# Two key tiles of half 8 go to the softmax denominators one by one on TensorE, without a sum on GpSimd

## The chip, the cores and the metric

The kernel runs on one core of a Trainium2 chip. The metric is the device time of one execution in microseconds (us), the median of several runs. The core has a matrix engine (TensorE, PE in the rows; its weight loads are PEld), a vector engine (VectorE, DVE), an activation engine (ScalarE, ACT), GpSimd (POOL) and a queue of transfers on SyncE (SP). Each runs its own instructions in program order and waits for the others by semaphores.

## What is computed

A gated cross-attention block and a gated feed-forward block over x (4 batches of 1024 rows, 512 columns), with 16 heads of 32 columns:

```
q = rope(layernorm(x));  k = rope(ctx);  v = ctx
scores = q . k / sqrt(32) + alibi bias
attn   = softmax(scores);  out = attn . v
x = x + tanh(g_xattn) * out
x = x + tanh(g_ffn) * ffn(layernorm(x))      # quantized gate, up and down projections
```

The softmax is computed as exponentials P, a numerator (P times v) and a denominator (the sum of P over the 1024 keys), which divides at the end. The change is in how the denominator is summed.

## The kernel before

The attention part works on 16 units of one batch and four heads, each cut in two **halves** of 512 queries: 32 halves, number 0 to 31. The 1024 keys of a half are 8 **tiles** of 128 keys, number 0 to 7, and each tile has a **step**: s = 0 to 7 in half hf, global number g = 8*hf + s. The order of the work is written out by hand: a class Step says for every g which jobs of which half each engine does, and every engine's program walks over the same list.

In a step TensorE computes the scores of this tile for four heads (L1066, f16, four column blocks of 32), the scores of an earlier-to-be-used tile for the row maxima (L1053, ten steps ahead, in two units of 1024 columns), and the numerator of the tile before (L1128, fp32). In the trace a step starts with the row `L1066 ... x8`. ScalarE turns scores into P (L1308, one instruction a head, into a ring of six P buffers). VectorE reduces the two units of scores to maxima (L1533); a bank of PSUM that it has not yet read holds back TensorE's next L1053 into that bank.

The denominator of a half is a product of summed P with a small matrix of zeros and ones, `pick`, which sums over the 128 keys of a tile (`denominators`, L1099, 16 fp32 matmuls, each two instructions in the trace, so x32). What is summed first:

- Sum 0: GpSimd adds tiles 0 and 1 at step 1 (L2186), then a transfer with addition from GpSimd's queue adds tile 2 (L2162, issued at step 3). TensorE takes it at step 6.
- Sum 2: GpSimd adds tiles 3 and 4 at step 4, a transfer adds tile 5 (step 6). TensorE takes it at step 10, that is step 2 of the next half.
- Sum 1: GpSimd adds tiles 6 and 7 at step 7. TensorE takes it at step 9, step 1 of the next half, ahead of that step's numerator.

In a half for which `direct(hf)` is true, sum 1 doesn't exist: TensorE takes tile 6 out of its P buffer at step 7 (behind the numerator) and tile 7 at step 9 (ahead of the numerator). Before the change these are the even halves from 18 to 28.

Beside the sums GpSimd does the rotary embedding (`rope`: L2010, L2017, L2018, L2028) for the unit after next, adds x to the output (L2172, step 5), works out deviations (L2055) and, in later halves, parts of the weight quantization. ScalarE copies the denominator out at step 3 of the next half (L1345); that row marks each half once. TensorE transposes the half's results at step 4 of the next half (L1135, L1139).

In the names, Ps are the buffers of the sums, P those of the exponentials, and g_sum, a_exp, pe_den count GpSimd's sums, ScalarE's exponentials and TensorE's denominators. ScalarE may write a P buffer again when what read its tile is done: for tiles 6 and 7 that is g_sum, and pe_den in a direct half.

Of the kernel before, what the change touches and what calls it, by code (L numbers as in the profile page):

```python
# [113 lines left out]

def direct(hf):

    return hf % 2 == 0 and 18 <= hf < 30


def sums(hf):  # L120

    return 2 if direct(hf) else 3


def den_steps(hf):

    return {0: 6, 6: 7, 7: 9, 2: 10} if direct(hf) else {0: 6, 1: 9, 2: 10}
# [1112 lines left out]
def scalar_program(e, K):  # L1240
# [51 lines left out]
    def exponent(hf, kt, h):  # L1292
        pb = (8 * hf + kt) % NP
        n = 8 * hf + kt
        e.wait_ge(K.pe_score, score_no(hf, kt, h))
        if h == 0 and n >= NP:
            m = n - NP
            e.wait_ge(K.pe_pv, m + 1)
            hm, km = m // 8, m % 8
            if hm < NHALF - 1 and km > 5 and direct(hm):  # L1300
                e.wait_ge(K.pe_den, den_no(hm, km))
            elif hm < NHALF - 1 and km % 3 < 2:
                e.wait_ge(K.g_sum, sum_no(hm, (0, 2, 1)[km // 3]))
            elif hm < NHALF - 1:
                e.wait_ge(K.d_acc[km // 3], 16 * hm + 16)
            else:
                e.wait_ge(K.v_sum, m // 2 - 4 * (NHALF - 1) + 1)
        e.activation(K.Pb[pb][:, h, :], K.score[h % 2], ACT.Exp, scale=SCALE / (QPOW * KPOW)).then_inc(K.a_exp, 1)  # L1308
# [951 lines left out]
```

## Time and profile before

| | |
|---|---|
| median of 3 runs | 1728.41 us (1728.23 to 1728.67) |
| the profiled execution, its own time | 1728.73 us |
| its span, first to last instruction | 1726.9 us |
| mean granted TensorE clock | 0.979 |
| attention part, by the denominators' copies (L1345) | 89.72 us (half 0) to 894.43 us (half 31) |
| step 1 of half 8 to step 1 of half 10 | 266 to 320 us |

The page of the profile gives busy shares over the whole span, of which the attention part is the first half; what binds in the attention part must be read from its own stretch. TensorE's busy time hides how matmuls overlap, so the distance between the starts of its rows says more than their durations.

### The profile page before, as it was taken

The page shows a single profiled execution, that of the slowest core. Times are in us where ns is not written, and L with a number is a line of the kernel's source. Part 1 is how long each engine was busy: PE and PEld are TensorE (multiplying, and loading weights), DVE is VectorE, ACT ScalarE, POOL GpSimd, SP SyncE. Part 2 cuts the span into 40 slices and gives each one's busy share as a digit, 9 for nine tenths or more (in the row PEclk, how much of TensorE's full clock was granted, in tenths as well). Part 3 has the DMA queues.
Part 4 walks back from the last instruction along what each step waited for, and adds up shares of the span by engine and source line. Part 5 has one row for each costly group of instructions (what it writes and reads, how often), then busy time and mean ns, then how long its engine had stood idle before and what let it go on. Part 6 is the DMA issues. An engine that isn't in the chain of part 4 may idle for free. (4 is left out here: it accounts for less than half of the span.)

```text
span 1726.9 us, 42023 instructions
## 1 busy us (share of the span) xinstructions
PE 1593.0 (92%) x17245; PEld 692.4 (40%) x17245; DVE 1443.0 (84%) x2039; ACT 1206.7 (70%) x1938; POOL 810.1 (47%) x493
## 2 busy tenths in 40 slices
PE   3999999999999999999969999999999950999999
PEld 0244444344334444444435444444444420444444
DVE  7899999999999989889857999868899989755541
ACT  3788888888889889998753332329996988754450
POOL 4799999999999999997830110200000000000000
PEclk9999999999999999999999999999999985999999
DMA  6678888888789797878478898649998999976661
GB/s 157 161 155 181 166 174 179 174 170 173 157 177 181 156 177 168 171 152 161 99 173 226 255 270 262 213 161 326 343 350 266 323 356 385 287 256 226 216 214 61
DMA packets 376337, 365.11 MB, mean 211 GB/s; under 512 B 217776, under 2 KB 288816, under 8 KB 368208
## 3 DMA queue, kind: packets, MB, share of 16 engines
q1 hardware_dynamic: 367216, 297.41, 61.7%
q0 software_dynamic: 8928, 65.02, 18.7%
q8 instruction: 135, 2.21, 0.5%
q14 instruction: 58, 0.48, 0.1%
HBM read 150.93 MB, written 95.42 MB: 143 GB/s over the span
## 5 line engine op out<-in xcount | busy, mean ns | idle before, releaser
L1533 DVE TENSOR_REDUCE cm<-quad 128x1 f16<-128x1024 f32 x512 | 600.3, 1214 | 52.6 <-PE quad L1053 52.1
L1308 ACT ACTIVATE P<-quad 128x512 f32<-128x512 f32 x1024 | 556.8, 598 | 119.6 <-PE quad L1066 108.7
L2186 POOL TENSOR_TENSOR Ps<-P,P 128x2048 f32<-128x2048 f32 x87 | 405.9, 4666 | 60.5 <-ACT P L1308 60.5
L1066 PE MATMUL quad<-QA,KA 101*32 101x512 f16 x4096 | 360.1, 384 | 8.1 <-ACT P L1308 6.1
L1053 PE MATMUL quad<-KA,QA 100*32 100x512 f16 x4096 | 334.5, 390 | 32.9 <-DMA QA<-S 16.9
L1128 PE MATMUL quad<-P,cg 128*32 128x512 f32 x2048 | 264.7, 592 | 0.0
L1158 PE MATMUL quad<-x_hl,Wg 128*128 128x512 f16 (+1 forms) x1200 | 248.9, 371 | 0.6 <-DVE x_hl L1852 0.6
L1158 PE MATMUL quad<-x_hl,Wu 128*128 128x512 f16 x1152 | 248.8, 380 | 0.0
L1219 PE MATMUL quad<-Wd,oh 128*128 128x512 f16 x768 | 228.8, 380 | 0.9 <-ACT oh L1502 0.9
L1066 PEld LDWEIGHTS quad<-QA,KA 101*32 101x32 f16 x4096 | 104.9, 95 | 247.0 <-ACT P L1308 218.8
L1053 PEld LDWEIGHTS quad<-KA,QA 100*32 100x32 f16 x4096 | 104.3, 96 | 181.3 <-DVE cm L1533 88.8
L1158 PEld LDWEIGHTS quad<-x_hl,Wg 128*128 128x128 f16 x1200 | 117.3, 98 | 132.7 <-issue 1.5
L1158 PEld LDWEIGHTS quad<-x_hl,Wu 128*128 128x128 f16 x1152 | 112.6, 98 | 136.0
L1392 ACT ACTIVATE ev<-quad 128x1024 f32<-128x1024 f32 x89 | 90.1, 1013 | 106.7 <-PE quad L1158 100.6
L1219 PE MATMUL quad<-Wd,ol 128*128 128x512 f16 x384 | 145.8, 380 | 0.2 <-DVE ol L1967 0.2
L2129 POOL TENSOR_TENSOR wq<-wl,wsc 128x512 f32<-128x512 f32 x36 | 43.1, 1197 | 211.9 <-DVE wl L1688 211.9
L1837 DVE TENSOR_REDUCE mxt<-ev 128x1 f32<-128x1024 f32 x89 | 108.1, 1215 | 35.9 <-ACT ev L1392 35.5
L1988 DVE SCALAR_TENSOR_TENSOR xr<-quad,qs,xr 128x512 f32<-128x512 f32 x32 | 23.9, 750 | 110.3 <-PE quad L1219 105.3
L1219 PEld LDWEIGHTS quad<-Wd,oh 128*128 128x128 f16 x768 | 75.1, 98 | 91.9 <-ACT oh L1502 1.4
L1502 ACT ACTIVATE oh<-oq 128x512 f16<-128x512 int16 x96 | 60.0, 625 | 67.3 <-DVE oq L1962 47.0
L1099 PE MATMUL quad<-Ps,pick 128*32 128x128 f32 x2912 | 96.4, 273 | 7.6 <-POOL Ps L2186 4.3
L1099 PEld LDWEIGHTS quad<-Ps,pick 128*32 128x32 f32 x2912 | 80.3, 110 | 56.5 <-issue 45.1
(181 smaller groups left out, 1964.7 us busy)
## 6 DMA issues: line engine op xcount, KB each, us to landing
Ps<-P POOLq DMA_DIRECT2D x62, 1024.0 KB, 8.0
gate_scratch<-ev SPq DMA_DIRECT2D x48, 512.0 KB, 3.9
gt<-gate_scratch SPq DMA_DIRECT2D x48, 512.0 KB, 5.3
ud<-up_scratch SPq DMA_DIRECT2D x96, 256.0 KB, 3.6
up_scratch<-ev SPq DMA_DIRECT2D x42, 512.0 KB, 4.4
x_words<-up_scratch SPq DMA_DIRECT2D x39, 512.0 KB, 7.8
gated_scratch<-gq SPq DMA_DIRECT2D x48, 256.0 KB, 4.1
gd<-gated_scratch SPq DMA_DIRECT2D x96, 128.0 KB, 4.2
```

Of the source, the lines that this page charges most:

```text
L1053: mm = e.matmul(K.bank(use, c)[j:j + 32, :], K.QA[p % 2][0:100, 4 * qc + qt, h, j:j + 32], K.KA[p % 2][0:100, 4 * c:4 * c + 4, h, :], star ...
L1066: mm = e.matmul(K.score[h % 2][j:j + 32, :], K.KA[p % 2][0:101, kt, h, j:j + 32], K.QA[p % 2][0:101, 4 * qc:4 * qc + 4, h, :], start=True, ...
L1099: mm = e.matmul(K.den[32 * h:32 * h + 32, :], K.pick[:, qt, :], src[:, h, 128 * qt:128 * qt + 128], start=n == order[0] and qt == 0, stop= ...
L1128: mm = e.matmul(K.num[32 * h:32 * h + 32, :], K.cg[(p + 1) % 4][:, kt, 32 * h:32 * h + 32], K.Pb[before.g % NP][:, h, :], start=kt == 0, s ...
L1158: mm = e.matmul(K.quad[z][:, o:o + w], W(part, c), K.x_hl[:, x, c0:c0 + w], start=n == 0, stop=n == 11)
L1219: mm = e.matmul(ps, o[k][:, ot, sl], K.Wd[r][:, ot, :], start=ot == m == 0, stop=ot == OT - 1 and m == 2)
L1308: e.activation(K.Pb[pb][:, h, :], K.score[h % 2], ACT.Exp, scale=SCALE / (QPOW * KPOW)).then_inc(K.a_exp, 1)
L1392: e.activation(dst, src, ACT.Copy).then_inc(K.a_ev, 1)
L1502: e.activation(K.oh[ch % 2][:, ot, :], K.oq[n % 2][:, :], ACT.Copy).then_inc(K.a_oh, 1)
L1533: e.tensor_reduce(cm[:, col:col + 1], K.quad[UNIT["max", hm, u] % 2][:, :], AX.X, ALU.max).then_inc(K.v_max, 1)
L1837: e.tensor_reduce(K.mxt[:, col:col + 1], src, over, ALU.max, apply_absolute_value=True).then_inc(K.v_mx, 1)
L2186: e.tensor_tensor(K.Ps[n][:, :, :], K.Pb[(st.g - 1) % NP][:, :, :], K.Pb[st.g % NP][:, :, :], ALU.add).then_inc(K.g_sum, 1)
```

## The change

Half 8 becomes a direct half too.

```diff
 def direct(hf):
 
-    return hf % 2 == 0 and 18 <= hf < 30
+    return hf == 8 or hf % 2 == 0 and 18 <= hf < 30
 
 
 def sums(hf):
 
     return 2 if direct(hf) else 3
 
 
 def den_steps(hf):
 
     return {0: 6, 6: 7, 7: 9, 2: 10} if direct(hf) else {0: 6, 1: 9, 2: 10}
```

On TensorE, at step 7 of half 8, the difference is one group of 16 matmuls more (P_94 holds tile 6, cg is v; the rows count a matmul once):

```order
 L1066 MATMUL quad<-QA_86,KA_88 32x512 x4
 L1128 MATMUL quad<-P_94,cg_84 32x512 x4
+L1099 MATMUL quad<-P_94,pick 32x128 x16
 L1066 MATMUL quad<-QA_86,KA_88 32x512 x8
 L1053 MATMUL quad<-KA_89,QA_87 32x512 x12
```

The group stands behind the numerator of tile 6 and ahead of the scores of half 9's first tile.

On TensorE two steps later, at step 1 of half 9, a group reads another buffer (Ps_98 is sum 1, P_141 holds tile 7, P_90 is tile 0 of half 9):

```order
 L1053 MATMUL quad<-KA_89,QA_87 32x512 x4
 L1066 MATMUL quad<-QA_86,KA_88 32x512 x4
-L1099 MATMUL quad<-Ps_98,pick 32x128 x16
+L1099 MATMUL quad<-P_141,pick 32x128 x16
 L1128 MATMUL quad<-P_90,cg_84 32x512 x4
 L1066 MATMUL quad<-QA_86,KA_88 32x512 x8
```

Its place and its size stay; what it waits for is no longer GpSimd's sum.

On GpSimd, at step 7 of half 8, the sum goes (Ps_99 is sum 2, t is the rotary embedding, Ps_97 is sum 0 of half 9):

```order
 L2162 DMA Ps_99<-P_93 128x2048
 L2028 TENSOR_TENSOR t_136<-t_136,t_137 128x1024
-L2186 TENSOR_TENSOR Ps_98<-P_94,P_141 128x2048
 L2010 TENSOR_TENSOR t_135<-xn,cos 128x1024
 L2186 TENSOR_TENSOR Ps_97<-P_90,P_91 128x2048
```

All behind it on GpSimd moves up by one place. VectorE, ScalarE and SyncE have the same instructions in the same order.

## Rows read from the trace of the kernel before

**Rows 1.** The page, part 1: busy us, share of the span, instructions
```profile
PE 1593.0 (92%) x17245; PEld 692.4 (40%) x17245; DVE 1443.0 (84%) x2039; ACT 1206.7 (70%) x1938; POOL 810.1 (47%) x493
```

**Rows 2.** Windows of 26 and 27 us over half 8 and half 9
```profile
core 0: us, PE busy (x) PEld busy (x) DVE busy (x) ACT busy (x) POOL busy (x), PEclk, DMA share, GB/s
261.00:287.00 26.00, 24.90 (x421) 10.37 (x417) 24.08 (x34) 22.58 (x44) 25.20 (x11) 1.00 0.96 187
287.00:313.00 26.00, 24.64 (x417) 10.51 (x413) 25.17 (x43) 21.05 (x40) 24.49 (x19) 1.00 0.71 156
```

**Rows 3.** Timeline of TensorE, end of half 8: start us, us, instruction, [idle before]
```profile
283.90 1.04 PE L1099 MATMUL quad<-Ps,pick 128*32 128x128 f32 x32
284.77 0.61 PE L1066 MATMUL quad<-QA,KA 101*32 101x512 f16 x8
...
287.79 0.60 PE L1066 MATMUL quad<-QA,KA 101*32 101x512 f16 x8
...
289.08 0.40 PE L1053 MATMUL quad<-KA,QA 100*32 100x512 f16 x4 [0.25 <-DVE cm L1533]
...
290.82 0.61 PE L1066 MATMUL quad<-QA,KA 101*32 101x512 f16 x8
...
294.55 0.61 PE L1066 MATMUL quad<-QA,KA 101*32 101x512 f16 x8
```

**Rows 4.** Timeline of TensorE in direct half 20, steps 7 to 1
```profile
601.69 0.61 PE L1066 MATMUL quad<-QA,KA 101*32 101x512 f16 x8
...
604.62 1.04 PE L1099 MATMUL quad<-P,pick 128*32 128x128 f32 x32
605.50 0.61 PE L1066 MATMUL quad<-QA,KA 101*32 101x512 f16 x8
...
608.16 0.61 PE L1066 MATMUL quad<-QA,KA 101*32 101x512 f16 x8
```

**Rows 5.** Timeline of GpSimd, half 8's last sum and half 9
```profile
287.88 4.62 POOL L2186 TENSOR_TENSOR Ps<-P,P 128x2048 f32<-128x2048 f32 x1 [1.09 <-ACT P L1308]
292.46 2.39 POOL L2010 TENSOR_TENSOR t<-xn,cos 128x1024 f32<-128x1024 f32 x1
294.81 4.56 POOL L2186 TENSOR_TENSOR Ps<-P,P 128x2048 f32<-128x2048 f32 x1
...
301.81 0.79 POOL L2162 DMA_DIRECT2D Ps<-P  x1
...
315.21 4.82 POOL L2186 TENSOR_TENSOR Ps<-P,P 128x2048 f32<-128x2048 f32 x1
```

**Rows 6.** Timeline of TensorE in half 9: its two waits
```profile
310.88 1.08 PE L1099 MATMUL quad<-Ps,pick 128*32 128x128 f32 x32 [1.04 <-DMA Ps<-P]
...
320.08 1.08 PE L1099 MATMUL quad<-Ps,pick 128*32 128x128 f32 x32 [0.47 <-POOL Ps L2186]
```

**Rows 7.** Timeline of ScalarE, exponentials of half 9's tile 1
```profile
292.80 1.10 ACT L1308 ACTIVATE P<-quad 128x512 f32<-128x512 f32 x2
```

**Rows 8.** Timeline of GpSimd in direct half 20
```profile
611.32 4.59 POOL L2186 TENSOR_TENSOR Ps<-P,P 128x2048 f32<-128x2048 f32 x1 [2.62 <-ACT P L1308]
```

**Rows 9.** The sums' buffers, 299.5 to 313 us: transfer to landing
```profile
DMA to landing us min/median/max: 8.9/8.9/8.9
```

**Rows 10.** Timeline of VectorE in the same stretch
```profile
289.53 2.35 DVE L1533 TENSOR_REDUCE cm<-quad 128x1 f16<-128x1024 f32 x2
...
312.31 0.87 DVE L1766 BATCH_NORM_STATS2 st<-x2s 128x6 f32<-128x128 f32 x4 [0.55 <-POOL x2s L2172]
```

**Rows 11.** ScalarE's copies of the denominators, halves 7, 8, 23 and 24
```profile
273.78 0.28 ACT L1345 ACTIVATE denT<-quad 128x128 f32<-128x128 f32 x1
299.50 0.28 ACT L1345 ACTIVATE denT<-quad 128x128 f32<-128x128 f32 x1
...
695.61 0.28 ACT L1345 ACTIVATE denT<-quad 128x128 f32<-128x128 f32 x1
721.82 0.28 ACT L1345 ACTIVATE denT<-quad 128x128 f32<-128x128 f32 x1
```

## The prediction

> **What bounds the kernel now.** I began with the busy shares of the page [rows 1]. They put TensorE first (92%) and GpSimd at 47%, and say nothing useful here: GpSimd has work only in the attention part. So I went to windows of the stretch around the change [rows 2]. There GpSimd is busy for 25.20 of 26.00 us over half 8 and 24.49 over half 9, VectorE for 24.08 and 25.17, TensorE for 24.90 and 24.64. The reader should see three engines that are nearly full, each of which can be late only a few tenths of a microsecond before it holds up another. Sizes of instructions alone then decide nothing. What counts is how the few gaps between them open and close, and the timelines give those.
>
> TensorE at the end of half 8 [rows 3]: step 7 runs from 284.77 to 287.79 (3.02 us), step 0 of half 9 from there to 290.82 (3.03 us), step 1 to 294.55 (3.73 us). A group of denominators takes 284.77 - 283.90 = 0.87 us between starts (not the 1.04 us of the row, which is the overlapped duration), so step 1 without its group is 2.86 us. What is a step with no wait at all? Step 0 of direct half 20 has no group in it and takes 608.16 - 605.50 = 2.66 us [rows 4]. TensorE thus loses 0.36 us in step 7, 0.37 in step 0 and 0.20 in step 1, and the row at 289.08 says to whom: to VectorE, which has not yet read a bank of maxima [rows 3].
>
> GpSimd [rows 5]: it waits 1.09 us for tile 7 before the sum at 287.88, which takes 4.62 us. From then on there is no gap: the rotary embedding at 292.46, sum 0 of half 9 at 294.81, the transfer with addition at 301.81, sum 1 of half 9 from 315.21 to 320.03. Two of these are waited for in half 9 by TensorE [rows 6]: it stands 1.04 us for the transfer (at 310.88) and 0.47 us for sum 1 (at 320.08). So through half 9 it is GpSimd that sets the end, which is what makes a sum taken off it interesting.
>
> **The change, part by part.**
>
> *Removed: sum 1 of half 8 on GpSimd, 4.62 us [rows 5].* Little of that can be passed on. The rotary embedding behind it can move up by nearly all of it, but sum 0 of half 9, the next but one, needs the exponentials of half 9's tile 1. Before, ScalarE ended them at 292.80 + 1.10 = 293.90 [rows 7], so GpSimd, which began at 294.81, was 0.91 us late and no more. In direct half 20, where the sum is already gone, the same instruction at 611.32 indeed waits, 2.62 us, for ScalarE [rows 8], and begins 611.32 - 608.16 = 3.16 us after TensorE's step 1 [rows 4, 8]. I use this 3.16. With TensorE's step 1 where it was (290.82) sum 0 would start at 293.98, 0.83 us earlier. This is the ceiling of the gain.
>
> *Added: one group of denominators on TensorE at the end of step 7.* The same group out of a P buffer takes 605.50 - 604.62 = 0.88 us in half 20 [rows 4]. It waits for nothing: the numerator just ahead of it reads the same tile. Step 0 then starts at 288.67 rather than 287.79. A TensorE that is later no longer waits for VectorE: 0.37 us of the delay is absorbed in step 0 and 0.20 in step 1. The 0.36 lost in step 7 lies ahead of the group and stays. So step 1 starts at 290.82 + 0.88 - 0.37 = 291.33, and step 2 at 294.55 + 0.88 - 0.57 = 294.86: 0.31 us late. If none of it were absorbed it would be 0.88, if all were, 0.
>
> *Changed source at step 1:* the group there reads tile 7 and not the sum. Same size, same place, and no row shows TensorE standing for the sum there; nothing.
>
> *The release of P buffers for ScalarE* now comes from TensorE (at about 288.7 and in step 1) and not from GpSimd at 292.50. These buffers are written again at steps 4 and 5 of half 9, later than either. Nothing, and if that cover were gone it would cost only what TensorE's groups are late.
>
> *Sum.* Sum 0 of half 9 starts at 291.33 + 3.16 = 294.49, against 294.81: 0.32 us earlier. What follows it on GpSimd has no gap, so the transfer goes out at 301.49. It landed 8.9 us after issue [rows 9]; the wait at 310.88 ends at 310.56. TensorE, which was there at 310.88 - 1.04 = 309.84, is there at 310.15 and still waits 0.41. The delay of TensorE has thus vanished in a wait that was there anyway, and that is why it costs nothing in the end. VectorE is pushed in step 0 by less than TensorE (it started on that step's maxima at 289.53, 1.74 us behind TensorE's start), and waits 0.55 us for GpSimd's L2172 at 312.31 [rows 10], which takes up the push. At 320.08 TensorE waits for sum 1, now 0.32 earlier; even with no gain at the transfer TensorE could be there at 320.08 - 0.47 = 319.61, ahead of 319.76 [rows 6]. From there all engines stand 0.32 us earlier and do the same work as before, to the end. The profiled execution would take 1728.73 - 0.32 = 1728.41 us; the median of the runs shown, 1728.41, is 0.32 below that execution, so the prediction is 1728.41 - 0.32 = **1728.09 us**, rounded 1728.1. Measurement tells 0.2% (3.5 us) from no change, so this is no change.
>
> *A rule weighed.* The row: between the groups of denominators TensorE's steps follow each other at 2.66 us, one after another, in which nothing waits [rows 4], so 0.88 us more of matmuls that find no gap are 0.88 us later. The Trainium skill, page "Perfetto Trace Analysis", section "Identifying the Most-Contended Engine", says that a matmul share is no measure of TensorE's headroom, and that the share of weight loads is one. Here that is 40%. Read so, TensorE would have room and the added group would cost nothing; the sum by the page would be the ceiling, -0.83 us, and 1727.58. I weigh this against the row as the third rival below.
>
> **The rivals.**
>
> *Whole sum passed on (3%).* If GpSimd alone set the pace, 4.62 us would go: 1723.8 us. For it: GpSimd is the fullest engine over half 8 [rows 2] and has no gap for 32 us behind the sum [rows 5]. Against it: the 293.90 of the exponentials [rows 7] and the 2.62 us that half 20 waits [rows 8].
>
> *The exponentials come later than I reckon (12%), the slower side.* The removal gains only while TensorE's step 1 starts before 294.81 - 3.16 = 291.65. If the delay is not absorbed (VectorE falls late with TensorE, and releases its banks later) step 1 starts at 291.70 and the gain is -0.05. More than that: direct half 24 lasts 721.82 - 695.61 = 26.21 us, and half 8 lasts 299.50 - 273.78 = 25.72 [rows 11]. If being direct is what costs these 0.49 us, GpSimd's sum 0 is as late and the result is 1728.41 + 0.49 = 1728.90. Against it: halves around 24 have more work of weights on GpSimd and VectorE, so the comparison is loose.
>
> *TensorE's added group is hidden in whole (17%).* Its step 1 starts where it did, and GpSimd gains the ceiling: 1728.41 - 0.83 = 1727.58. This needs VectorE to be the one that paces steps 7 to 1 with more to spare than the 0.57 us that I count.
>
> *Nothing (20%).* GpSimd's own instructions differ by more than the gain: the same L2186 takes 4.56 and 4.82 us within half 9 [rows 5], as it meets other work or not. A shift of its neighbours can eat 0.3 us: 1728.4.
>
> **How the numbers follow.** My forecast has 46%; with the four rivals that is 98%. The last 2% are for a shift that I can't place in the long transfer-heavy part behind the attention. Cases from 1727.58 to 1728.90 hold 95%; the medians' own scatter (0.44 us between runs) and the rounding of the cases add some tenths on each side: 1726.9 to 1729.2. The faster side by over 0.2% (below 1724.95) needs the whole sum passed on, 3%; slower by over 0.2% (above 1731.9) has only the unplaced remainder, 2%; no change 95%.
>
> **What the profile of the changed kernel would show.** A group `P,pick` at about 287.8 and the next step at 288.67; no wait for VectorE at 289; step 2 of half 9 at 294.86. GpSimd idle for about 3 us around 291, for ScalarE, and sum 0 of half 9 at 294.49. The transfer's wait in TensorE about 0.4 us, ending near 310.56; the wait for sum 1 near 319.76, and the copy of half 9's denominators 0.3 us earlier than before. The prediction is wrong if sum 0 starts after 294.81, if the shift at 320 us is not the shift at the end, or if GpSimd doesn't wait at all in the gap.

## The result, and the profile after

| | before | changed |
|---|---|---|
| median of the timed runs | 1728.81 us (1727.58 to 1731.75, 15 runs) | 1732.53 us (1729.64 to 1735.82, 15 runs) |
| ratio, 95% interval | | 1.0019 [1.0013, 1.0026] |
| profiled execution, own time and span | 1728.73 and 1726.9 us | 1731.29 and 1729.5 us |

The changed kernel is 3.7 us slower by the medians, and the interval of the ratio does not reach 1. The forecast was 1728.1 us, no change, range 1726.9 to 1729.2. The three runs shown ahead of the prediction were close to each other (0.44 us); over 15 runs the same kernel spreads by 4.2 us, so the measured effect is clear and not large.

Half 8 itself did what was predicted. The two traces stand 0.43 us apart when half 8 begins (copy of half 7's denominators at 274.21, before 273.78 [rows 11]), so all positions below are to be read against that. Timeline of TensorE in the changed kernel, steps 7 to 1, the answer to [rows 3]:

```profile
285.20 0.61 PE L1066 MATMUL quad<-QA,KA 101*32 101x512 f16 x8
...
288.22 1.04 PE L1099 MATMUL quad<-P,pick 128*32 128x128 f32 x32
289.09 0.60 PE L1066 MATMUL quad<-QA,KA 101*32 101x512 f16 x8
...
291.76 0.61 PE L1066 MATMUL quad<-QA,KA 101*32 101x512 f16 x8
...
295.29 0.61 PE L1066 MATMUL quad<-QA,KA 101*32 101x512 f16 x8
```

The new group takes 289.09 - 288.22 = 0.87 us, and step 2 starts at 295.29, which is 294.55 + 0.43 + 0.31: TensorE is 0.31 us late, as worked out. GpSimd, the answer to [rows 5]:

```profile
294.91 4.59 POOL L2186 TENSOR_TENSOR Ps<-P,P 128x2048 f32<-128x2048 f32 x1 [3.86 <-ACT P L1308]
```

It waits for ScalarE and starts 3.15 us after step 1 (3.16 predicted), 0.33 us earlier than before once the 0.43 are taken off. TensorE's two waits in half 9, the answer to [rows 6]:

```profile
310.78 1.08 PE L1099 MATMUL quad<-Ps,pick 128*32 128x128 f32 x32 [0.26 <-DMA Ps<-P]
...
320.28 1.08 PE L1099 MATMUL quad<-Ps,pick 128*32 128x128 f32 x32 [0.49 <-POOL Ps L2186]
```

The second is at 320.08 + 0.43 - 0.23: the place where the gain was to arrive shows 0.23 us of the 0.32. Up to here there is no loss at all.

The loss is in halves that the change doesn't touch. The copies of the denominators give the length of each half. ScalarE in the changed kernel, halves 11, 12, 17, 18, 19 and 20:

```profile
379.75 0.28 ACT L1345 ACTIVATE denT<-quad 128x128 f32<-128x128 f32 x1
406.19 0.28 ACT L1345 ACTIVATE denT<-quad 128x128 f32<-128x128 f32 x1
...
538.78 0.30 ACT L1345 ACTIVATE denT<-quad 128x128 f32<-128x128 f32 x1
565.59 0.28 ACT L1345 ACTIVATE denT<-quad 128x128 f32<-128x128 f32 x1
592.34 0.28 ACT L1345 ACTIVATE denT<-quad 128x128 f32<-128x128 f32 x1
619.94 0.28 ACT L1345 ACTIVATE denT<-quad 128x128 f32<-128x128 f32 x1
```

The same rows of the kernel before:

```profile
379.42 0.28 ACT L1345 ACTIVATE denT<-quad 128x128 f32<-128x128 f32 x1
405.14 0.28 ACT L1345 ACTIVATE denT<-quad 128x128 f32<-128x128 f32 x1
...
537.77 0.29 ACT L1345 ACTIVATE denT<-quad 128x128 f32<-128x128 f32 x1
563.99 0.28 ACT L1345 ACTIVATE denT<-quad 128x128 f32<-128x128 f32 x1
590.75 0.28 ACT L1345 ACTIVATE denT<-quad 128x128 f32<-128x128 f32 x1
616.66 0.28 ACT L1345 ACTIVATE denT<-quad 128x128 f32<-128x128 f32 x1
```

Half 12 lasts 26.44 us against 25.72, half 18 26.81 against 26.22, half 20 27.60 against 25.91: together 3.0 us. TensorE stands in these halves for the transfer with addition that completes sum 0. Its timeline in the changed kernel, halves 12 and 20:

```profile
391.23 1.08 PE L1099 MATMUL quad<-Ps,pick 128*32 128x128 f32 x32 [1.19 <-DMA Ps<-P]
...
604.15 1.08 PE L1099 MATMUL quad<-Ps,pick 128*32 128x128 f32 x32 [1.57 <-DMA Ps<-P]
```

Neither wait is in the trace of before. Halves 18 and 20 last as long as in before, within 0.04 us, in copy_before and in few (few is described below and loses no time); half 18 is 0.37 us longer in pool_only. Half 12 is no sign of the change: few, which has the time of before, has the wait too, and its half 12 lasts 26.75 us (pool_only: 26.84). TensorE in few:

```profile
390.80 1.08 PE L1099 MATMUL quad<-Ps,pick 128*32 128x128 f32 x32 [1.51 <-DMA Ps<-P]
```

So single halves of single traces have to be read with care. Still, why do transfers far behind the edit land later? Nothing in their data flow has changed. What has changed for everything behind half 8 is its place in the instruction stream, and the page says how that stream reaches the core: by transfers of its own. The row of queue 8 of the page, part 3, of the kernel before:

```profile
q8 instruction: 135, 2.21, 0.5%
```

and of the changed kernel:

```profile
q8 instruction: 136, 2.23, 0.5%
```

2.21 MB in 135 packets is 16 KB a packet. TensorE has 2 x 17245 rows, matmuls and weight loads [rows 1], which makes 64 bytes for each and 256 instructions for a packet, if the packets are TensorE's. They are by their rhythm: from 89.72 to 894.43 us the trace has 102 packets of this queue beside 25958 matmuls and weight loads, from 894.43 to 1400 us 19 beside 4701, so 254 and 247 instructions a packet, while the time between packets goes from 7.9 to 26.6 us. (Another instruction queue, q14, has 58 packets before and after.) TensorE passes 421 + 417 matmuls and loads in 26 us [rows 2], so 256 instructions are some 7.9 us, and 64 more instructions bring every later fetch some 2.0 us forward against the work around it. Both times are estimates from those rows. The idea can be tested: by 64 instructions that do nothing, anywhere ahead.

A simpler way from instructions to time can be ruled out at once: TensorE does not stand for its own instructions. Of its waits over 0.15 us between 85 and 900 us, each one in the traces of before and of the changed kernel ends with a semaphore of another engine or of a transfer.

### The profile page after: what moved, and what is told of

The parts are those of the page before. It is cut to its first block and busy times, and to the rows that moved or that the text cites. A ratio compares the mean times of both kernels' runs of the same rounds, so it can differ in the third digit from the quotient of the medians.

```text
span 1729.5 us, 42085 instructions
## 1 busy us (share of the span) xinstructions
PE 1596.5 (92%) x17277; PEld 694.6 (40%) x17277; DVE 1443.5 (83%) x2039; ACT 1207.3 (70%) x1938; POOL 806.0 (47%) x492
## 5 line engine op out<-in xcount | busy, mean ns | idle before, releaser
L1533 DVE TENSOR_REDUCE cm<-quad 128x1 f16<-128x1024 f32 x512 | 600.3, 1214 | 56.6 <-PE quad L1053 55.9
L2186 POOL TENSOR_TENSOR Ps<-P,P 128x2048 f32<-128x2048 f32 x86 | 401.4, 4667 | 67.5 <-ACT P L1308 67.5
```

Source lines behind the costliest of these rows:

```text
L1533: e.tensor_reduce(cm[:, col:col + 1], K.quad[UNIT["max", hm, u] % 2][:, :], AX.X, ALU.max).then_inc(K.v_max, 1)
L2186: e.tensor_tensor(K.Ps[n][:, :, :], K.Pb[(st.g - 1) % NP][:, :, :], K.Pb[st.g % NP][:, :, :], ALU.add).then_inc(K.g_sum, 1)
```

## The experiments

Kernels of one group ran on one chip, beside the kernel before; the groups ran on different chips. The theories by their letters: A, scatter of the landings between executions alone; B, a cause in the change, B1 the missing sum, B2 the added group or its place in the stream; F, the phase of TensorE's instruction fetches, which the added 64 instructions shift; T, the 0.88 us of TensorE's time in half 8.

### One half of the change at a time

**copy_before**: no edit. **after_again**: the changed kernel, no edit.

> The kernel before, unchanged, timed against itself. It tells how far a ratio of two identical kernels can stand from 1, and gives a second trace, in which the waits of TensorE for the transfers with addition can be set against those of the first. Theory A (the change costs nothing at its own place, and the 3.7 us between the medians come from transfers that land at different times in different executions): ratio within 0.9985 to 1.0015, and the waits of TensorE for the transfers sum to 2 to 6 us, in other halves than in the first trace. Theory B (the change itself makes it slower): ratio within 0.9995 to 1.0005, waits as in the first trace, 3.1 us.

> The changed kernel again, unchanged. Theory A (scatter of the landings): ratio between 0.999 and 1.002, and the halves that are longer than before in its trace are not 12, 18 and 20 again. Theory B (a cause in the change): ratio 1.0013 to 1.0026 as measured, and the same halves 12, 18 and 20 are longer by 0.6 to 1.7 us.

**pool_only** (the changed kernel; the denominators of half 8 leave out tile 6, and ScalarE does not wait for its buffer; an excerpt):

```diff
 def den_steps(hf):
+    if hf == 8:
+        return {0: 6, 7: 9, 2: 10}
```

> Half 8 without the sum of tiles 6 and 7 on GpSimd, and without the added group on TensorE (tile 6 is left out of the denominators of half 8). Account of the prediction: sum 0 of half 9 starts 0.83 us earlier than before, median 0.8 us below before. Theory A: ratio 0.998 to 1.001. Theory B1 (what costs is the sum that is missing on GpSimd, by shifting its transfers against those of SyncE's queue): 1.0013 to 1.0026. Theory B2 (what costs is the added group on TensorE or its place in the instruction stream): 0.9995.

**pe_only** (the changed kernel; GpSimd still makes the sum, which only ScalarE waits for, before it writes the buffers again; an excerpt):

```diff
 def sums(hf):
-    return 2 if direct(hf) else 3
+    return 2 if direct(hf) and hf != 8 else 3
```

> Half 8 with both groups on TensorE as after the change, but GpSimd still makes the sum, which nothing reads. Account of the prediction: TensorE 0.31 us late at step 2 of half 9, taken up by its wait of 1.04 us for the transfer unless GpSimd is late too: 0 to +0.3 us. Theory B1 (missing sum on GpSimd costs): ratio 1.000 to 1.0002. Theory B2 (added group on TensorE or its place in the instruction stream): 1.0013 to 1.0026.

| kernel | TensorE instructions added | median, us | ratio [95%] |
|---|---|---|---|
| before, beside them | 0 | 1729.52 | |
| copy_before | 0 | 1728.94 | 0.9996 [0.9988, 1.0005] |
| pool_only | 0 | 1729.20 | 0.9996 [0.9987, 1.0005] |
| after_again | 64 | 1731.66 | 1.0012 [1.0003, 1.0021] |
| pe_only | 64 | 1732.25 | 1.0020 [1.0009, 1.0031] |

The copy bears out that the comparison finds no difference where there is none. Its trace was expected to repeat the waits of before if theory B holds, and did not: TensorE waits 4.1 us in all for the transfers between 85 and 900 us and not 3.1, and its halves 10, 11 and 22 are 0.35 to 0.49 us longer. So the landings do scatter between executions of one kernel. As the whole cause theory A falls: the intervals of after_again and pe_only do not reach 1. The sum on GpSimd is not the cause (B1 falls): with it gone and TensorE's count unchanged, nothing is lost. With it kept and the group added, the loss is there. (In pe_only's trace one wait for a transfer, 2.73 us in half 12, is followed by a granted clock of 0.57 from 393 to 397 us, and that half lasts 29.62 us.) pool_only also confirms the ceiling of the gain at its place. GpSimd in pool_only:

```profile
294.32 4.57 POOL L2190 TENSOR_TENSOR Ps<-P,P 128x2048 f32<-128x2048 f32 x1 [3.35 <-ACT P L1312]
```

Its half 8 begins at 274.12, so the sum starts 20.20 us behind that, before 294.81 - 273.78 = 21.03: 0.83 us earlier, exactly the 0.83 of the prediction. In the medians this gain can't be told from nothing (1729.20 beside 1729.52). Of after_again's trace the expectation was too strict: half 18 is longer again (26.80), half 12 and half 20 only by 0.28 and 0.30 us. What returned more closely was not the halves but some of the landings, below.

### Is it the time of the added group, or its 64 places in the stream?

**pad64**: the kernel before, with 16 small fp32 matmuls in the idle time at the start, 64 instructions.

```diff
     mm.then_inc(K.pe_bias, 1)
+    for i in range(16):
+        e.matmul(K.quad[3][0:32, 512:544], ident[:, 0:32], ident[:, 0:32], start=True, stop=True)
```

> The kernel before, with 64 more TensorE instructions (16 small fp32 matmuls, 32 weight loads and 32 matmuls) in the idle time at the very start, where TensorE waits for its first operands; half 8 as before. Theory F (the added group moves all later TensorE instructions by 64 places in their stream, so that the fetches of 16 KB, 256 instructions each, meet other transfers with addition): from half 13 on the landings are those of the changed kernel (sum 0 of half 18 in 9.0 us and not 7.0, sum 2 of half 15 in 7.6 and not 9.7, sum 2 of half 29 in 9.0 and not 7.3), and the ratio is 1.000 to 1.002. Theory T (the 0.88 us of TensorE in half 8 do the harm): landings as before, ratio 0.9995 to 1.0005.

**few**: the kernel before, with as much TensorE time in half 8's place, in 8 instructions.

```diff
     for st in STEPS:
+        if st.g == 72:
+            e.wait_ge(K.a_exp, score_no(9, 0, 0) - 2)
+            for i in range(4):
+                e.matmul(K.score[0][0:32, :], K.KA[0][0:100, 0, 0, 0:32], K.QA[0][0:100, 0:4, 0, :], start=True, stop=True)
```

> The kernel before, with TensorE kept busy for about 0.85 us ahead of the scores of half 9's first tile by 4 f16 matmuls of 512 columns (8 instructions in place of 64), whose result is overwritten. Theory F: landings as in the kernel before, ratio 0.9995 to 1.0005, at most +0.3 us locally. Theory T: as the changed kernel, 1.001 to 1.0025.

**after_pad192** and **after_pad256**: the changed kernel with the loop of pad64, 48 and 64 matmuls.

> The changed kernel with 192 more TensorE instructions in the idle time at the start, so that behind half 8 the stream is 256 places later than in the kernel before: one fetch more, and the same phase. Theory F: from half 9 on the landings are those of the kernel before (sum 0 of half 18 in 7.0 us), and the ratio 0.998 to 1.001, unless the halves 1 to 8, whose phase is now 192 places off, lose something of their own. Theory T: 1.001 to 1.0025, as the changed kernel.

> The changed kernel with 256 more TensorE instructions at the start: the phase of the fetches is everywhere as in the changed kernel. It is the control for what the padding itself costs. Theories F and T both: 1.001 to 1.0025, landings as in the changed kernel. If the padding costs by itself, more than that.

| kernel | added ahead of half 9 | median, us | ratio [95%] |
|---|---|---|---|
| before, beside them | 0 | 1729.26 | |
| few | 8 | 1729.11 | 0.9999 [0.9990, 1.0008] |
| pad64 | 64 | 1733.61 | 1.0018 [1.0009, 1.0026] |
| after_pad256 | 256 + 64 | 1732.67 | 1.0014 [1.0005, 1.0022] |
| after_pad192 | 192 + 64 = 256 | 1731.88 | 1.0011 [1.0002, 1.0019] |

The pair pad64 and few is the core of the study. pad64 leaves half 8 alone, adds 64 idle instructions at the very start, and has the whole loss. few puts about the same time of work in the very place (its half 8 lasts 26.03 us, the changed kernel's 26.04) and has none. Theory T falls. What pad64's trace, one execution of 1730.40 us, does not show is the loss in the same halves. Its halves 18 and 20 last as long as in before, within 0.04 us, and the first transfer of half 18 landed in 7.5 us where 9.0 was expected; the longer ones are half 2 (by 1.12 us) and half 5 (by 0.51). The expected landings of half 15 (7.6) and half 29 (9.1) came.

The traces show what the count does to a landing. The second transfer of half 29 (sum 2) is far from any edit and from the halves that wait. For it, the traffic in the 7 us from its issue, of the kernel before (packets, MB, share of 16 engines; KB, us to landing):

```profile
q0 software_dynamic: 144, 1.05, 73.3%
q1 hardware_dynamic: 298, 0.26, 10.9%
...
Ps<-P POOLq DMA_DIRECT2D x1, 1024.0 KB, 7.3
```

and of the changed kernel:

```profile
q0 software_dynamic: 143, 1.05, 73.2%
q1 hardware_dynamic: 292, 0.26, 10.8%
q8 instruction: 1, 0.02, 0.8%
...
Ps<-P POOLq DMA_DIRECT2D x1, 1024.0 KB, 9.0
```

The data traffic is the same; there is one packet of instructions more, and the landing is 1.7 us later. The packet is not new: in before it starts 7.3 us after the issue, when the transfer has landed, and in the changed kernel 7.0 us after it. pad64, the same window:

```profile
q8 instruction: 1, 0.02, 0.8%
Ps<-P POOLq DMA_DIRECT2D x1, 1024.0 KB, 9.1
```

Over all of the first 14 traces (all but those of the last section of experiments) this one transfer takes, by what is added ahead of it: 0 or 8 instructions (before, copy_before, pool_only, few) 7.2 to 7.4 us; 256 (after_pad192, direct_2_8, direct_10_16) 7.3; 64 (after, after_again, pe_only, pad64, direct_10) 8.7 to 9.1; 320, that is 64 and one whole fetch (after_pad256), 9.1; 128 (pad128) 7.0. Others follow the same classes, in either direction: the first transfer of half 30 takes 7.5 to 7.7 and 8.5 us, the second of half 15 8.4 to 9.7 and 7.6 to 7.7. The landing repeats every 256 instructions. How can a packet of 16 KB among 1 MB cost up to 2 us? The Trainium skill, page "DMA: Bandwidth & Descriptors", section "Why a DMA increments its semaphore by 16 and not by 1", says that for a transfer from GpSimd's queue all 16 engines count the semaphore up, each behind its own data, and that only the full 16 means that all has landed. The traces agree: the 15th of the 16 increments of this transfer comes 7.0 us after the issue in before and in the changed kernel alike, the 16th at 7.3 and at 9.0. One part in 16 is late. That it is late because the packet stands ahead of it on the same engine is argued from this, not shown: the traces don't say which engine an increment or a packet belongs to.

A packet in the window is no rule by itself. The first transfer of half 18 in before has one too, 6.75 us after its issue, and lands in 7.0 us; in the changed kernel the packet starts at 6.98 and the landing is 9.0:

```profile
q8 instruction: 1, 0.02, 1.0%
Ps<-P POOLq DMA_DIRECT2D x1, 1024.0 KB, 7.0
```

What seems to count is when it comes. Of the 868 transfers in the 14 traces, which took 6.7 to 11.6 us (median 8.1), the 62 in which a packet of queue 8 starts 3 to 6 us after the issue all took 8.4 us or more (median 9.3).

Do later landings make the time? The attention part, from the copy of half 0's denominators to that of half 31's, follows TensorE's waits for the transfers (between 85 and 900 us): from 806.2 us with 2.0 us of waits (direct_2_8) and 804.7 with 3.1 (before) to 810.4 with 8.5 (pad128), correlation 0.89 over the 14 traces. But the traces do not separate the kernels as the medians do. With 0 or 8 instructions added the waits are 3.1, 4.1, 4.2 and 5.0 us, with 64 added 3.6, 3.7, 6.0, 6.0 and 6.3.

after_pad192 gave the landings of before from half 9 on, as theory F says, but not the time. Two things blur it: halves 4 and 8, now in another phase, are 1.24 and 0.67 us longer than in before beyond what the change adds, and in its trace TensorE's clock rises late, so that half 0 ends at 91.81 us and not at 89.72. Windows of after_pad192 (busy us and count of TensorE, its weight loads, VectorE, ScalarE and GpSimd, then the granted clock, the DMA share and GB/s):

```profile
40.00:50.00 10.00, 8.35 (x64) 1.12 (x64) 9.81 (x13) 2.00 (x2) 9.75 (x7) 0.50 0.63 159
50.00:60.00 10.00, 9.28 (x84) 2.85 (x88) 8.02 (x8) 4.87 (x9) 3.13 (x2) 0.50 0.87 200
```

and of the kernel before:

```profile
40.00:50.00 10.00, 8.34 (x64) 1.12 (x64) 9.81 (x13) 2.00 (x2) 9.84 (x6) 1.00 0.63 157
50.00:60.00 10.00, 8.30 (x92) 2.54 (x96) 8.98 (x8) 5.39 (x10) 3.65 (x3) 1.00 0.83 201
```

and of after_again, without any padding, and after_pad256, with the longest:

```profile
50.00:60.00 10.00, 9.66 (x84) 2.89 (x88) 8.02 (x7) 5.26 (x9) 2.72 (x2) 1.00 0.97 207
50.00:60.00 10.00, 9.00 (x104) 2.56 (x96) 8.64 (x8) 6.49 (x13) 3.73 (x3) 0.77 0.91 212
```

From 50 to 60 us TensorE gets through 84 matmuls in after_pad192 where it got through 92 in before. The padding is not the reason: after_again without padding gets through 84 too, after_pad256 through 104. The traces record the rise to the full level at 54.0 to 61.0 us, early or late with padding and without it, so it belongs to the single execution. (The 1.00 of before in the first of these windows is no record: the trace of before has none ahead of 55.5 us. 64 matmuls take 8.34 us there and 8.35 beside a 0.50, so TensorE was at its lower level in both.) Whether the halves in another phase explain the ratio of after_pad192 stayed open, and it was replaced by kernels without padding.

### The phase restored without padding, and moved

```diff
 def direct(hf):
-    return hf % 2 == 0 and 18 <= hf < 30
+    return hf in (2, 4, 6, 8) or hf % 2 == 0 and 18 <= hf < 30     # direct_2_8
+    return hf in (10, 12, 14, 16) or ...                           # direct_10_16
+    return hf == 10 or ...                                         # direct_10
```

pad128 is pad64 with 32 matmuls.

> Halves 2, 4, 6 and 8 direct: four groups of 64 TensorE instructions more, so that from half 9 on the stream is 256 places later, one whole fetch, and the fetches have the phase of the kernel before. Theory F: landings from half 13 on as in the kernel before (sum 2 of half 29 in 7.3 us, sum 0 of half 30 in 7.6); ratio 0.998 to 1.0010, below the 1.0012 to 1.0019 of the changed kernel. Theory T (each group on TensorE costs by itself, what half 8 alone cost): four times 0.0012 to 0.0019, ratio 1.005 to 1.008.

> Halves 10, 12, 14 and 16 direct in place of 8: the phase of the fetches is that of the kernel before up to half 9 and from half 17 on. Theory F: landings from half 17 on as in the kernel before, ratio 0.998 to 1.001. Theory T: 1.005 to 1.008.

> Half 10 direct in place of half 8: the same 64 instructions, 16 steps later. Theory F: landings as in the changed kernel from half 13 on, ratio 1.0005 to 1.002. A theory by which half 8 is special (its deviations on GpSimd and aggregates on VectorE in half 9): ratio 0.9995 to 1.0005.

> The kernel before with 128 more TensorE instructions in the idle time at the start, half a fetch. Theory F says that the time depends on the phase and not which way: between 0.998 and 1.003, with landings that are neither those of before nor those of the changed kernel. If padding at the start costs by itself in proportion to its length, it is above the 1.0018 of 64 instructions.

| kernel | added, from where | median, us | ratio [95%] |
|---|---|---|---|
| before, beside them | 0 | 1729.45 | |
| direct_2_8 | 64, 128, 192, from half 9 on 256 | 1729.74 | 1.0004 [0.9994, 1.0013] |
| direct_10 | 64 from half 11 on | 1732.42 | 1.0016 [1.0008, 1.0025] |
| direct_10_16 | 64 to 192 in halves 11 to 16, then 256 | 1733.47 | 1.0030 [1.0007, 1.0052] |
| pad128 | 128 everywhere | 1734.37 | 1.0032 [1.0021, 1.0043] |

Four groups like the one of the change, in direct_2_8, cost less than one alone in direct_10, 1729.74 against 1732.42 us on the same chip, and no difference to before is measured. Under theory T the ratio would be 1.005 to 1.008. Half 8 is not special either, half 10 does the same. direct_10_16 missed its expectation. Its landings are those of before from half 17 on and its halves 17 to 30 last as long, but its halves 12 and 14, in the phases between, last 27.23 and 26.87 us against 25.72, where their own added groups account for 0.32 each. So a phase is not good or bad by itself; what counts is which transfers the fetches meet while it lasts. (One of its twelve executions took 2433.69 us and one 1755.30, for which there is no trace; the median does not feel them, but the second is in the ratio and widens its interval.) pad128 costs more than pad64, as theory F allows; a cost of the padding by its length would do that too, but then after_pad256, with 256 idle instructions, should cost more than the changed kernel, and it does not (1.0014).

### By which wait it reaches the time

Three phases again, with TensorE taking sum 0 at step 7 and not at 6 in every half but the last, so that a late landing is covered:

```diff
-    return {0: 6, 6: 7, 7: 9, 2: 10} if direct(hf) else {0: 6, 1: 9, 2: 10}
+    return {0: 7, 6: 7, 7: 9, 2: 10} if direct(hf) else {0: 7, 1: 9, 2: 10}
```

> The kernel before, with TensorE taking sum 0 of every half at step 7 and not at step 6 (the last half aside), 2.7 us later, so that a transfer that lands in 9.0 us and not in 7.0 is still there in time. Theory F (late landings reach the time through TensorE's wait for sum 0 at step 6): the waits for transfers, 3 to 4.5 us in sum before, fall below 1 us, the time falls by 1 to 3 us: ratio 0.998 to 0.9995. If landings cost in another way, 0.9995 to 1.001.

> The changed kernel with sum 0 taken at step 7 in every half. Theory F: it loses nothing to the other phase of the fetches, and is within 1 us of late_before, ratio 0.998 to 0.9998. If the loss of the changed kernel comes by another way than TensorE's wait for sum 0, it stays 2 to 3 us above late_before.

> The kernel with 128 more TensorE instructions at the start, the slowest phase seen (1.0032), with sum 0 taken at step 7. Theory F: within 2 us of late_before, ratio 0.998 to 1.0005 (the throttled clock of the start may cost up to 1 us). By another way: 1.002 to 1.003.

| phase | sum 0 at step 6, us | at step 7, us | ratio [95%] at 7 | TensorE's waits in the trace, 85 to 900 us, for transfers, at 6 and at 7 | for VectorE's L1533 |
|---|---|---|---|---|---|
| before | 1729.45 | 1736.89 | 1.0039 [1.0026, 1.0051] | 3.1 and 0 us | 7.4 and 21.9 us |
| changed | 1732.53 | 1737.38 | 1.0052 [1.0039, 1.0065] | 6.0 and 0 | 7.4 and 21.9 |
| 128 added | 1734.37 | 1735.52 | 1.0038 [1.0026, 1.0050] | 8.5 and 0 | 7.8 and 21.9 |

The kernel before took 1729.92 us beside the three at step 7. Those at step 6 are from other groups. late_before ran five times, of which one took 9413.45 us, without a trace; it is in the median, which would be 1736.49 without it, and not in the ratio. The other two ran six and five times.

The waits for the transfers are gone in all three, as expected. For 128 added the loss is gone with them: at step 6 it stood 0.0032 above before, at step 7 it is level with late_before. For the changed kernel it is not resolved: 0.0013 above late_before, with intervals of 0.0013 on each side, fits none of its loss and all of it. Its trace has a stretch of its own, a granted clock of 0.50 from 420.8 to 424.0 us, and half 13 lasts 28.69 us there and 27.00 in late_before. And moving the sum did more than cover the landings: TensorE now waits 14.5 us longer for VectorE, which could also take up a delay that comes another way. So these runs fit theory F and do not single out the wait at step 6.

The other half of the expectation, that all three get faster, was wrong: they are 6 to 8 us slower than before. Timeline of TensorE in late_before, half 8:

```profile
285.54 0.60 PE L1066 MATMUL quad<-QA,KA 101*32 101x512 f16 x8
286.96 1.12 PE L1053 MATMUL quad<-KA,QA 100*32 100x512 f16 x12 [0.82 <-DVE cm L1533]
```

Without a group in step 6 TensorE comes early and waits 0.82 us for VectorE, and the group then stands behind that wait: each of the even halves 2 to 14 lasts 26.04 us and not 25.72, the same 0.32 that the added group cost half 8. The direct halves, where two groups now stand together in step 7, lose more, 0.69 to 0.96 us each.

## Why the prediction was wrong

- **The group's price, and how much VectorE's gaps absorb** (0.88 us, of which 0.57 absorbed): right. 0.87 and 0.31 us late at step 2.
- **Sum 0 of half 9 starts 3.16 us behind step 1, 0.32 us earlier; ceiling 0.83**: right, 0.33 in the changed kernel and 0.83 in pool_only.
- **The gain at 320 us**: right in sign and place, 0.23 and not 0.32. The wait for the transfer there was 0.26, not 0.41, as the transfer landed in 8.7 us and not in 8.9.
- **The step that failed** is the one behind it: "From there all engines stand 0.32 us earlier and do the same work as before, to the end." The shift at 320 us was -0.23, that of the medians +3.7: one of the signs of being wrong that the prediction named. The engines do the same work, but TensorE's instructions are 64 places later in their stream. The term "added: one group" was counted by its time, and not by its instructions. Their count moves all later fetches, and with them the landings of transfers for which TensorE waits. That the count is the cause is shown by pad64 (the loss without the group, 1.0018), few (the group's time without the loss, 0.9999) and direct_2_8 (four groups, a whole fetch, 1.0004); that it moves landings, by the 14 traces. That these landings make up the loss through TensorE's waits is in part argued: the attention part grows with the waits, but single traces of the two kinds overlap, and of the three kernels with sum 0 at step 7 only the one with 128 added loses its loss clearly.
- **The rivals**: none was it. The slower one, late exponentials, did not happen. The one that rested on weight loads at 40%, that the added group is hidden in whole, did not either: TensorE was 0.31 us late at step 2. The 2% left for "a shift that I can't place in the long transfer-heavy part behind the attention" named the wrong part. That part, from the last copy of denominators to the end of the span, is 1726.9 - 894.43 = 832.5 us before and 1729.5 - 897.72 = 831.8 after.
- **The range**: it took the 0.44 us between three runs for the scatter. 15 runs spread by 4.2 us. That alone did not make it wrong: the median of these 15, 1728.81, lies inside it.

What stays open. The traces account for a part of the medians: from the copy of half 0's denominators to that of half 31's it is 804.7 us before (89.72 to 894.43), 806.2 in copy_before, and 808.3 and 806.8 in the two traces of the changed kernel, a mean difference of 2.1 us, while the medians differ by 2.1 to 3.7. With pool_only and few (806.4 and 807.3) on the one side and pe_only, pad64 and direct_10 (810.5, 806.9 and 807.9) on the other it is 2.0. The profiled executions of the changed kernel (1731.29 and 1729.28) were below its medians, so the typical loss may be larger; no trace shows one. A long wait can cost more than itself, as the lower clock behind the 2.73 us in pe_only shows; how often that happens in the executions without a trace is not known. Halves 6 and 7 are 0.35 and 0.31 us longer in the changed kernel's trace, ahead of the edit. pool_only and few show nearly the same (half 6 26.12 and 26.11), with no loss in time, so it isn't the change. Which of the 16 engines delays the landing was not tried.

## What to carry to other kernels

Where transfers land just in time, count the instructions that an edit adds as well as their time, and test with a padding of the same count where the engine idles: if the padding alone has the effect, the edit's own merit is not what was measured. An edit whose gain is a few tenths of a microsecond can't be judged in such a kernel at one phase alone. A wait that sits on a landing with less than 2 us to spare is where such shifts can come in, but moving it has its own price.

## What the runs showed of the hardware that was not expected

- TensorE's instructions come during the execution, in packets of 16 KB, one for some 250 matmuls and weight loads. Each transfer of 1024 KB with such a packet starting 3 to 6 us after its issue took at least 8.4 us (62 of 868; the median of all is 8.1).
- A late landing can be one part in 16: the 15th increment of the semaphore comes at 7.0 us, the 16th at 7.3 in before and at 9.0 in the changed kernel (second transfer of half 29).
- Some landings are nearly a fingerprint of the program: the second transfer of half 29 repeats within 0.2 us (0 or 8 instructions added) and 0.4 us (64 added), on different chips, and comes back after 256 TensorE instructions. Others are not: with 64 added, the first of half 20 landed in 9.3 us in one trace and in 7.7 to 7.8 in four.
- With the same work up to there, TensorE's full clock (2.4 GHz) is on record from 54.0 us in one execution (few) and from 60.9 in another (after_again), and half 0 ends at 88.14 and 91.06 us. In the first window of before the granted clock reads 1.00 where the matmuls' own duration (8.34 us for 64, as beside a 0.50) shows the lower level; at the start of a trace the duration is to be believed.
- A wait of 2.73 us for a transfer (pe_only, half 12) was followed by 0.57 of the clock from 393 to 397 us. In late_after the clock was 0.50 from 420.8 to 424.0 us behind a wait of 1.56 us; in late_before it stayed at 1.00 behind the same wait.
